# The bias of the second output product carried by idle rows of its weights, and a 64-unit product made 128 rows wide

## The reference, cut to what matters

```python
x = L0_attn_query                                    # (16, 1024, 512)
x = layernorm(x + attn(x, ...))                      # sparsemax attention over 32 learned keys, 16 heads
# the part that the change touches:
s = einsum('btd,dm->btm', x, Win) + bin_             # 512 -> 64 units
h = relu(s[..., None] * W1 + b1)                     # 16 inner values of each unit
g = einsum('btmh,mh->btm', h, W2) + b2               # back to 64 units
out = einsum('btm,md->btd', g, Wout) + bout          # 64 -> 512
x = layernorm(x + out)
```

## Time and profile before

| | us |
|---|---|
| times of 3 runs | 1375.8, 1378.0, 1378.3 |
| median | 1378.0 |
| the profiled execution | 1377.4 |
| its span, first to last instruction | 1375.6 |

### The profile page before, as it was taken

The page is one execution under the profiler, slowest core; times in us unless marked ns, Lnnn a source line. Parts: engine busy times, 40 slices in busy tenths (PEclk is TensorE's granted clock), DMA queues, the critical chain, the costliest instruction groups (busy, mean ns, idle before and its releaser), DMA issues. The chain is left out here.

```text
span 1375.6 us, 28046 instructions
## 1 busy us (share of the span) xinstructions
PE 1267.5 (92%) x6990; PEld 833.1 (61%) x6990; DVE 1129.1 (82%) x4600; ACT 1158.1 (84%) x2621; POOL 687.4 (50%) x1672
## 2 busy tenths in 40 slices
PE   7980989999999999999999999999999999799953
PEld 6650566666666666666666666666666666455431
DVE  2986888888888888888888888888888898866764
ACT  2670766789999999999999999999999999767773
POOL 1330333345555555556555555555555555556663
PEclk9995999999999999999999999999999999999975
DMA  5380676555655655655655665565565565568733
GB/s 182 91 216 16 168 224 214 182 174 181 215 186 191 215 193 185 213 196 187 209 199 184 208 203 186 203 211 188 193 214 190 188 215 185 200 196 290 252 98 69
DMA packets 91848, 258.31 MB, mean 188 GB/s; under 512 B 15731, under 2 KB 15731, under 8 KB 75286
## 3 DMA queue, kind: packets, MB, share of 16 engines
q1 hardware_dynamic: 91670, 256.39, 57.4%
HBM read 206.00 MB, written 50.33 MB: 186 GB/s over the span
## 5 line engine op out<-in xcount | busy, mean ns | idle before, releaser
L659 PE MATMUL bank<-G_sb,pT 128*128 128x512 f32 x1024 | 463.7, 596 | 2.4 <-ACT pT L754 2.4
L659 PEld LDWEIGHTS bank<-G_sb,pT 128*128 128x128 f32 x1024 | 185.7, 191 | 188.2 <-issue 185.5
L1070 DVE MAX8 top<-bank 128x8 f32<-128x32 f32 x2048 | 212.7, 182 | 39.9 <-issue 39.7
L466 POOL TENSOR_TENSOR shift_sq<-sum,per_row_sq 128x1 f32<-128x1 f32 x256 | 89.1, 348 | 281.1 <-DVE y_sb L946 278.3
L1108 DVE SCALAR_TENSOR_TENSOR acc<-hinge,w2c,acc 128x512 f32<-128x512 f32 x224 | 167.7, 749 | 65.6 <-ACT hinge L779 63.4
L767 ACT ACTIVATE unread<-y_sb,shift_sq 128x512 bf16<-128x512 f32 x256 | 184.0, 719 | 37.5 <-POOL minus_mean L468 37.2
L779 ACT ACTIVATE hinge<-s_sb,b1c,w1c 128x512 f32<-128x512 f32 x256 | 205.8, 807 | 0.2
L584 PE MATMUL bank<-A_hi,xT_hi 128*128 128x512 f32 x512 | 203.4, 397 | 0.0
L585 PE MATMUL bank<-A_lo,xT_hi 128*128 128x512 f32 x512 | 203.1, 397 | 0.0
L586 PE MATMUL bank<-A_hi,xT_lo 128*128 128x512 f32 x512 | 203.0, 397 | 0.0
L481 POOL TENSOR_TENSOR rstd<-ve,minus_half 128x1 f32<-128x1 f32 x256 | 153.1, 598 | 45.2 <-POOL ve L476 44.9
(11 more groups left out here) (128 smaller groups left out, 2510.0 us busy)
## 6 DMA issues: line engine op xcount, KB each, us to landing
G_sb<-G_of_heads SPq DMA_DIRECT2D x128, 1024.0 KB, 5.4
x_sb<-in_L_attn_query_dram SPq DMA_DIRECT2D x128, 256.0 KB, 4.7
y_sb<-in_L_attn_query_dram SPq DMA_DIRECT2D x256, 128.0 KB, 5.4
out_dram<-o_sb SPq DMA_DIRECT2D x256, 128.0 KB, 4.7
G_of_heads<-y_sb SPq DMA_DIRECT2D x64, 256.0 KB, 3.9
y_sb<-in_L_attn_Wk_dram SPq DMA_DIRECT2D x1, 1024.0 KB, 5.6
y_sb<-in_L_attn_Wq_dram SPq DMA_DIRECT2D x1, 1024.0 KB, 8.3
y_sb<-in_L_attn_Wv_dram SPq DMA_DIRECT2D x1, 1024.0 KB
```

Source lines behind the costliest of these rows:

```text
L466: nc.gpsimd.tensor_tensor(shift_sq[:, par:par + 1], total[:, par:par + 1], per_row_sq[:], ALU.mult).then_inc(s_mean, 1)
L659: mm = nc.tensor.matmul(o_ps[i % 2][:], pT[:, bass.ds(pair_place(turn, i) + (i % H * C + c) * P, P)], G_sb[:, i % GR, c, :], start=(c == 0 ...
L1070: mx = nc.vector.max(top8[:, h, :], z_ps[i % 2][:, h * S:(h + 1) * S])
```

## The change

It has two parts, and what they need in the set-up.

First, `bout` rides on the second pass of the output product. A new tile `second` holds the rounded 64 rows once more in its rows 0 to 63 and ones in rows 64 to 127. `Wout_lo` keeps the rest of `Wout` in rows 0 to 63 alone; of its other rows, which are zero, row 64 has the rounded `bout` and row 96 its rest. The pass of `pick_c` by `bout_rows` goes. ACT writes `second` with one more 64x512 copy behind the copy into `split` (semaphore `s_high`, for which PE waits at each group's first tile). The last group has a place in `A_lo` for it, which POOL fills with ones in slot 129 (`s_ones`).

Second, `Win` stands twice side by side in `Win_sb`, now 128 columns, loaded by two DMAs. s is four products of 128 weight columns by 128 tokens, and comes out on both halves of the partitions. One ACT copy of 128x128 replaces the four of 64x64, and the counts of `s_sc` go from 4 a tile to 1.

```diff
-        Win_sb = sb("Win_sb", [P, C, M])
+        Win_sb = sb("Win_sb", [P, C, P])
-        bout_rows = sb("bout_rows", [P, D], F32R)
+        second = sb("second", [P, GROUP * P], F32R)
...
-                (Win_sb[:], Win.rearrange("(c p) m -> p c m", p=P)),
...
+                    (Win_sb[:, :, half], Win.rearrange("(c p) m -> p c m", p=P)),
...
-            nc.gpsimd.memset(bout_rows[:].bitcast(F32), 0.0).then_inc(s_const, 1)
+            nc.gpsimd.memset(Wout_lo[:].bitcast(F32), 0.0).then_inc(s_const, 1)
+            nc.gpsimd.memset(second[:].bitcast(F32), 1.0).then_inc(s_const, 1)
...
+                if base + j == TILES + LAG_SCORE:
+
+                    pool.wait_ge(s_score, TILES)
+                    nc.gpsimd.memset(last_second.bitcast(F32), 1.0).then_inc(s_ones, 1)
...
                     for c in range(C):
-                        for t in range(2):
-                            tokens = slice(t * HALF, (t + 1) * HALF)
-                            mm = nc.tensor.matmul(s_ps[t * M:(t + 1) * M, 0:HALF], Win_sb[:, c, :],
-                                                  yT[:, c, tokens], start=(c == 0), stop=(c == C - 1))
+                        mm = nc.tensor.matmul(s_ps[:, 0:P], Win_sb[:, c, :], yT[:, c, :], start=(c == 0),
+                                              stop=(c == C - 1))
...
                         pe.wait_ge(s_lo, group_of(turn, i) + 1)
+                        pe.wait_ge(s_high, group_of(turn, i) + 1)
...
-                    nc.tensor.matmul(f[:], pick_c[:], bout_rows[:], start=True, stop=False)
-                    nc.tensor.matmul(f[:], parts[:, here], Wout_hi[:], start=False, stop=False)
-                    nc.tensor.matmul(f[:], parts[:, here], Wout_lo[:], start=False, stop=True).then_inc(s_f, 1)
+                    nc.tensor.matmul(f[:], parts[:, here], Wout_hi[:], start=True, stop=False)
+                    nc.tensor.matmul(f[:], high[:, here], Wout_lo[:], start=False, stop=True).then_inc(s_f, 1)
...
-                    for t in range(2):
-                        for half in (slice(0, M), slice(M, P)):
-                            rows = slice(t * M, (t + 1) * M)
-                            nc.scalar.activation(s_sb[half, par, q * P + t * HALF:q * P + (t + 1) * HALF],
-                                                 s_ps[rows, 0:HALF], ACT.Identity,
-                                                 bias=bin_sb[rows, :]).then_inc(s_sc, 1)
+                    nc.scalar.activation(s_sb[:, par, q * P:(q + 1) * P], s_ps[:, 0:P], ACT.Identity,
+                                         bias=bin_sb[:]).then_inc(s_sc, 1)
...
-                    nc.scalar.copy(split_of(lead)[0:M, :], both[0:M, :]).then_inc(s_hi, 1)
+                    nc.scalar.copy(split_of(lead)[0][0:M, :], both[0:M, :]).then_inc(s_hi, 1)
+                    nc.scalar.copy(split_of(lead)[1][0:M, :], both[0:M, :]).then_inc(s_high, 1)
...
-                    nc.vector.tensor_copy(bout_rows[0:1, :], bout_row).then_inc(s_c, 1)
-                    dve.wait_ge(s_c, 3)
-                    nc.vector.tensor_tensor(bout_rows[E:E + 1, :], bout_row, bout_rows[0:1, :].bitcast(F32),
-                                            ALU.subtract).then_inc(s_c, 1)
-                    nc.vector.tensor_copy(Wout_hi[:], Wout_sb).then_inc(s_ready, 1)
-                    dve.wait_ge(s_ready, C + 1)
-                    nc.vector.tensor_tensor(Wout_lo[:], Wout_sb, Wout_hi[:].bitcast(F32), ALU.subtract).then_inc(s_ready, 1)
+                    nc.vector.tensor_copy(Wout_hi[:], Wout_sb).then_inc(s_ready, 1)
+                    nc.vector.tensor_copy(rounded, bout_row).then_inc(s_c, 1)
+                    dve.wait_ge(s_ready, C + 1)
+                    nc.vector.tensor_tensor(Wout_lo[0:M, :], Wout_sb[0:M, :], Wout_hi[0:M, :].bitcast(F32),
+                                            ALU.subtract).then_inc(s_ready, 1)
+                    dve.wait_ge(s_c, 3)
+                    nc.vector.tensor_copy(Wout_lo[M:M + 1, :], rounded.bitcast(F32)).then_inc(s_c, 1)
+                    nc.vector.tensor_tensor(Wout_lo[M + E:M + E + 1, :], bout_row, rounded.bitcast(F32),
+                                            ALU.subtract).then_inc(s_c, 1)
```

More of the change, by code:

```diff
@@ L181, in build_kernel @@
         tau_some = sb("tau_some", [P, HPC])
-        last_split = A_hi[:, 0, :]
+        last_split, last_second = A_hi[:, 0, :], A_lo[:, 0, :]
         Wk_sb, Wv_sb, Wq_sb, Wo_sb = (y_sb[:, n * C:(n + 1) * C, :] for n in range(4))
@@ L190, in build_kernel @@
         bout_row = o_sb[0:1, 2, :]
+        rounded = split[0:1, :]
         K_blk = acc[:].rearrange("p (c n) -> p c n", c=C)
@@ L224, in build_kernel @@
         s_hinge, s_acc = sem("s_hinge"), sem("s_acc")
+        s_high, s_ones = sem("s_high"), sem("s_ones")
         s_upper, s_both, s_hi, s_lo = sem("s_upper"), sem("s_both"), sem("s_hi"), sem("s_lo")
@@ L287, in split_of @@
         def split_of(lead):
-            return last_split if lead == LAST else split[:]
+            return (last_split, last_second) if lead == LAST else (split[:], second[:])
         def so_far(turn, j, lag):
@@ L336, in group_of @@
             return turn * (UNROLL // GROUP) + i // GROUP
-        KEY_LOADS, Q_LOADS, WLOADS = 3, 2, 17
-        FILLS = 13 + S
+        KEY_LOADS, Q_LOADS, WLOADS = 3, 2, 18
+        FILLS = 14 + S
         CONSTS = FILLS + 4
@@ L641, in slot @@
                         if s_place(base + i - 1) is ys_ps:
-                            pe.wait_ge(s_sc, 4 * (base + i))
+                            pe.wait_ge(s_sc, base + i)
                     for c in range(C):
@@ L682, in slot @@
                         pe.wait_ge(s_lo, group_of(turn, i) + 1)
+                        pe.wait_ge(s_high, group_of(turn, i) + 1)
                         if isinstance(turn, int) and base + i == 0:
                             pe.wait_ge(s_ready, C + 2)
-                            pe.wait_ge(s_c, 4)
+                            pe.wait_ge(s_c, 5)
                     if not isinstance(turn, int) or base + i >= 1:
@@ L690, in slot @@
                     here = slice(i % GROUP * P, (i % GROUP + 1) * P)
-                    f, parts = f_place(base + i), split_of(base + i - i % GROUP)
-                    nc.tensor.matmul(f[:], pick_c[:], bout_rows[:], start=True, stop=False)
-                    nc.tensor.matmul(f[:], parts[:, here], Wout_hi[:], start=False, stop=False)
-                    nc.tensor.matmul(f[:], parts[:, here], Wout_lo[:], start=False, stop=True).then_inc(s_f, 1)
+                    f, (parts, high) = f_place(base + i), split_of(base + i - i % GROUP)
+                    if base + i == LAST:
+                        pe.wait_ge(s_ones, 1)
+                    nc.tensor.matmul(f[:], parts[:, here], Wout_hi[:], start=True, stop=False)
+                    nc.tensor.matmul(f[:], high[:, here], Wout_lo[:], start=False, stop=True).then_inc(s_f, 1)
                 if turn == 0 and j in (1, 2):
@@ L775, in make_hinge @@
                     if k == 0:
-                        act.wait_ge(s_sc, 4 * (lead + GROUP))
+                        act.wait_ge(s_sc, lead + GROUP)
                     if lead > 0 or k >= HR:
@@ L803, in slot @@
                         act.wait_ge(s_lo, lead // GROUP)
+                        act.wait_ge(s_high, lead // GROUP)
                     nc.scalar.copy(both[0:M, :], acc[M:P, :]).then_inc(s_upper, 1)
@@ L838, in slot @@
                         act.wait_ge(s_f, lead)
-                    nc.scalar.copy(split_of(lead)[0:M, :], both[0:M, :]).then_inc(s_hi, 1)
+                    if lead == LAST:
+                        act.wait_ge(s_ones, 1)
+                    nc.scalar.copy(split_of(lead)[0][0:M, :], both[0:M, :]).then_inc(s_hi, 1)
+                    nc.scalar.copy(split_of(lead)[1][0:M, :], both[0:M, :]).then_inc(s_high, 1)
                 if in_range(turn, j, LAG_X):
```

2 lines of the change are left out of this document (1 added, 1 removed).

## The result

The changed kernel takes **1360.9 us** in the median of four runs (1360.0 to 1361.6) against 1377.1 of the kernel before (1375.8 to 1378.3): a ratio of 0.988, with a 95% interval of 0.987 to 0.990. I had forecast 1382.4 and a range that began at 1375. It is faster by 16 us, where slower by 5 was expected.

The account below looks back on a forecast made before the run. PE was taken to bound the kernel from 228 to 1174 us, engine chains the end. 28.8 - 22.1 = +6.7, set-up +0.4, end -2.5 sum to +4.6 us, forecast 1382.4 us, range 1375 to 1390.

Parts of the forecast that it names:

- the price of s: PE, 228 to 1174 us: full-width s takes 0.89 us, 0.28 a tile more, adding 28.8 us over 103 tiles.
- the end: From 1174 us: fewer ACT copies start the late groups' chains earlier, -2.5 us in sum, between 0 and -6.
- the set-up: Before the slots: one more row copy on DVE, other additions hidden, +0.4 us, between 0 and 0.8.
- Part 1's pass: Output product on PE: dropping the `bout` pass saves 0.233 us in each of 95 slots, 22.1 us.
- rival 3: Output product on PE: the float32 to float32r step goes with L692, 9 us more saved, 1373.4 us; chance 0.06.
- L693 inherits the step: Output product on PE: the 0.1 us from float32 to float32r stays, moving from L692 to the next pass.
- An instruction taken from ACT is worth nothing: Up to 1174 us: PE hides ACT, so ACT's net saving of 0.78 us a tile gains no time.
- Rival 1: From 1174 us: shorter late waits and a vanished half-clock spell give -6 instead of -2.5, 1378.9 us; chance 0.20.
- Rivals 2 and 4: Full-width s on PE: 2, pace of half-width pairs, 1353.8 us, chance 0.06; 4, own 0.1 us starting step, 1392.7, 0.08.

Follow-up runs that it names:

- part 2 alone: The kernel before with wide `Win_sb`, s as full-width passes and one ACT copy, the `bout` pass kept: 1383.3 us, ratio 1.005.
- four-copy kernel: The kernel after, with s copied by ACT in four 64x64 pieces again instead of one 128x128 copy: 1375.7 us, ratio 1.000.
- kernel with the full-width passes in pieces: The kernel after, with its four full-width products of s split 2/1/1 around the output passes: 1360.6 us, ratio 0.988.
- kernel with the pieces: The kernel before, with its narrow s cut into four pieces of four passes standing between the output passes: 1473.9 us, ratio 1.070.

## Why the prediction was wrong, point by point

- **The failed step is the price of s, +0.28 us a tile.** It left out one term: the time that the narrow s costs in its neighbours' passes, which I put at nothing without a reason. In place of +0.28 the runs show +0.10 (part 2 alone). I took s's cost as the difference of its own rows, 0.89 - 0.61 = +0.28. The rows were right (0.89 in front of the transposes, 0.81 in front of L700). But the 0.61 was not the whole price of the narrow product. PE paid 0.093 more in the last pass of L659; and the first float32r pass behind it took its extra 0.1 with nothing given back ahead of it, where a full-width float32 product gives back 0.08 (0.81 instead of 0.89). Here is the ledger of a slot where s stands directly ahead of the output, from medians over the stretch, start to start (us):

```
                         before   after
product of G, 8 passes    3.529   3.436    -0.093
s                         0.615   0.810    +0.195
first output pass         0.338   0.313    -0.025
the other output passes   0.468   0.229    -0.239
sum                                        -0.162
```

In the slots where transposes stand between s and the output the time from L659 to L616 fell from 5.340 to 5.232, by 0.108: s itself costs 0.275 more there, L659 gives the same 0.093, and the transposes behind s, 0.411 before and 0.356 after, give 0.055. Half and half that is -0.135 a slot, and 94 slots make -12.7; the stretch shrank by 12.5. I had forecast +0.05 a slot. With 0.10 in place of 0.28 my sum loses 103 x 0.18 = 18.5 us and 1382.4 becomes 1363.9, an estimate; the end, 4.3 more saved than forecast, and the set-up, 0.9 dearer, bring it to 1360.5, where 1360.9 was measured.

- **How I missed it.** I took 8 passes of L659 at their spacing as L659's own, without looking whether its last pass was longer (seven take 0.43 each, the last 0.52). I costed the operation that goes by its own rows and never asked what its neighbours' rows contain on its account. The profile before held it: the 3.53 beside L659 and 8 x 0.43 = 3.44 do not agree.

- **Part 1's pass was right**: -0.233 forecast, -0.24 measured, and the first float32r pass kept its 0.31 to 0.34. That L693 inherits the step stands; rival 3 (1373.4) is out. But I missed its counterpart: at full width the last float32 pass gives back what the first float32r pass takes. In front of L692 there was no such gift, since the pass ahead of it was narrow.

- **"An instruction taken from ACT is worth nothing"** held for my own sum, in which PE got longer. In the real one it fails: with four copies of s the slot stops at 9.30 us, 0.03 under before, and the kernel gets 1 us out of the same work on PE. I had seen ACT at 97% and asked whether PE ever waits for it, not how much shorter PE could get before it would.

- **The end** was forecast at -2.5 and gave -6.8 (tiles 102 to 127 and the rest). The mechanism was right: at the late group PE waits 0.91 where it waited 1.43, and 0.9 was forecast; `L808` now waits for `acc`:

```profile
1249.57 0.76 DVE L1117 SCALAR_TENSOR_TENSOR acc<-hinge,w2c,acc 128x512 f32<-128x512 f32 x1 [0.66 <-ACT hinge L786]
1250.36 0.62 ACT L808 COPY both<-acc 64x512 f32<-64x512 f32 x1 [0.57 <-DVE acc L1117]
...
1254.36 0.50 PE L700 MATMUL bank<-Wout_hi,split 128*128 128x512 f32 x1 [0.91 <-POOL split L517]
```

The waits for L517 are 8.7 us in four places against 11.6:

```profile
PE bank L700 <- POOL split L517: 8.7, 4, 5.4
```

The size of the term was off: ACT's relief is worth 5.6 there, by the four-copy kernel, and not 3.3, and the packed slots between the groups gave about 1 back instead of costing 0.8 (with the four copies tiles 102 to 127 take 158.14 us against 159.18 before). Rival 1's size for the end, -6, was met, but the runs do not bear out its mechanism, a spell at half clock that goes. The trace after has one such short spell behind tile 102, where the one before has two. The kernel with the full-width passes in pieces has none before 1305 us (a granted clock of 1.00 from 1162.4 us on), and with 153.28 us between tiles 102 and 127 it is no shorter there than the kernel after, with 152.56.

- **The set-up** was forecast at +0.4. DVE's part is +0.3 (from 2.22 to 2.54 us); the start of tile 0 moved by 1.3. It lies at 226.7 to 228.0 in the profiles of four kernels with the set-up of before and at 228.0 to 229.5 in seven with that of after, so the kernel after starts later by some 1 us, but the two ranges touch, and where the part beyond DVE's 0.3 arises is not settled. ACT's busy time fell by 104 us (forecast 90 to 100), one copy takes 0.35 to 0.37 (0.37).

- **Rivals 2 and 4** are out: the full-width passes take 0.11 each as in L578, not the 0.076 of a narrow pair, and they pay nothing at their start. The 81 ns that the Trainium skill gives ("TensorE: Matmul & The Clock Gate", Back-to-back issue gap) for such a stream appear in none of these traces, which have 0.108 to 0.115 for float32 passes of 128 columns. By it, as in the prediction, the passes of s add 4 us and the time would be about 1358, an estimate; it lies nearer to the measured 1360.9 than mine, but by luck: the passes of s did not get cheap.

## What to carry to other kernels

Price an operation by the time from the start of the one before it to the start of the one after it, against the same stretch without it, and not by its own rows: small narrow products in a full-width stream cost 0.3 us here that stood in their neighbours' rows. Where a second engine stands at 97%, write down how much shorter the first may get before the second holds it, and ask whether the same change relieves the second engine: the first one's saving counts only as far as it does. And when an edit resizes a buffer, keep the places of all others the same before you read the result as the edit's.

## What the runs showed of the hardware

**Changes of width on PE.** An excursion from full-width passes to ones of 64 weight columns and back costs about 0.3 us at full clock: 0.093 in the pass ahead, 0.049 in the first pair, 0.094 behind the last and 0.098 in the next float32r pass (0.055 where transposes come next), by medians of spacing; 0.31 for each added one in the kernel with the pieces. At the count, with one weight column, it is 0.093 in the pass ahead and 0.058 in the first transpose behind. Why, the traces don't say. The pairs themselves take 0.058. The Trainium skill ("TensorE: Matmul & The Clock Gate", Part 3: Packing small matmuls) recommends side-by-side strips for small products; here the product by itself indeed took nearly half the time (0.47 us in eight pairs against 0.89 at full width), and of that 0.42 the edges took back 0.32, which leaves the 0.10 of part 2 alone. **Float32 and float32r at full width**: the change costs 0.08 in one pass and gives 0.08 in the other.

**Places in memory.** The float32r passes of the scores take 0.234 us, or 0.227 when the buffers behind the count's ones lie 480 bytes further on, in both kernels; 32 bytes did it for one of the three lines. Between before and after the buffers of the scores did not move, and their passes take 0.234 in both, so this has no share in the result. (`Wout_hi` and `Wout_lo` do lie 1024 bytes further on after the change, since `Win_sb` ahead of them has doubled; their passes behind the first take 0.23 us in both.) Of the operands of the score passes only `A_hi` and `A_lo` are declared behind the count's ones; `xT_hi` and `xT_lo` stand ahead of them and kept their places. Both shifts, 32 and 480 bytes, put `A_hi` and `A_lo` on multiples of 64 bytes, yet they gave different paces, so that alone does not decide it. Which of the moved buffers matters and why stays open. With the place and the full-width count the kernel takes 1351.0 us, 26 less than before.
